# Moving a PSUM copy ahead of a masked score on VectorE, and splitting a wait in front of the products with v

## The chip, the cores and the metric

The kernel runs on one core of a Trainium2 chip. The metric is the device time of one execution in microseconds. Three executions of the kernel before took 3114.57, 3116.45 and 3116.84 us; the median, 3116.45 us, is the time before.

## What is computed

The reference is a chain of four residual blocks on x of 16 sequences x 512 tokens x 256 channels: windowed attention with rotary embedding, an int8 linear layer, a linear attention, and a ternary feed-forward layer with a low-rank term. Only the first block is touched:

```python
q, k, v = split(x @ w_qkv)                    # 16 heads of 64
q, k = l2norm(q) * q_scale, l2norm(k) * k_scale
# windows of 128 queries; each sees the keys of its own, the previous and the next window
q, k = rotary(q * 8), rotary(k)               # rotary(t) = t * cos + rotate_half(t) * sin
sim = where(mask, -max, einsum('bwid,bwjd->bwij', q, k))
out = einsum('bwij,bwjd->bwid', softmax(sim), v) @ w_out
x = layernorm(x + out)
```

## The kernel before

Attention comes first (`run_attention`), sequence by sequence, and takes about 1.93 ms; the other layers follow and share nothing with it in time. The heads are taken in 8 pairs per sequence, 128 pairs in all. A sequence of 512 tokens has four windows (w = 0 to 3) of 128 queries; windows 0 and 3 see 256 keys, windows 1 and 2 see 384. All is fp32.

Every engine runs the same loop, `run_halves`: for each sequence b, each pair p, two halves u = 0 and 1. Half u handles the transposes of the softmax weights of windows w = 2u and w + 1 (global numbers i and i + 1) of its pair, the scores and softmax of the next two windows, and some projections of the pair after the next. Each engine has its own instruction queue, written out by hand: `pe_half`, `act_half`, `dve_half`, `pool_half`. Semaphores tie them together. For one window the work goes like this:

- TensorE computes the scores of both heads h into the PSUM banks SC[w % 2][h] (`pe_scores`, L292).
- VectorE adds the mask, scales, and takes the row extreme (`dve_mask_max`, L518), one instruction per head and a short read of the accumulator. I call it a masked score.
- ScalarE takes the exponential and the row sum (`act_exp`, L420), VectorE the reciprocals of both heads (`dve_reciprocals`, L525), GpSimd multiplies the weights by them (`pool_softmax`, L614).
- TensorE transposes the weights (`pe_transpose_weights`, L309): head 0 into the bank TP, from where ScalarE copies them to pt[0] (`act_evacuate_weights`, L426); head 1 into SC[0][0], or into the bank QK for window 3 of the pairs where `spare` is true (all but p = 0 and 6), from where VectorE copies them to pt[1] (`dve_evacuate_weights`, L530).
- When all four windows of pair n are in pt, TensorE multiplies with v at the head of the next pair's half u = 0 (`pe_values`, L318): 8 products, key block k = 0 to 3 by head, all added up in QK. Key block k needs the weights of windows k - 1 to k + 1 only, but both waits stand ahead of the first product.

Around it, in half u = 0 after the products with v: the next two windows' scores, the transposes of q of the next pair into QK (`pe_q_transpose`, L272; they wait for GpSimd's rotation L598), VectorE's copy of them (`dve_q_evacuate`, L510), the transposes of k into the same bank (`pe_k_transpose`, L279; they wait for that copy), ScalarE's copy of them (L415). VectorE also rotates the projections (`dve_rotate`, L497 and L498, after ScalarE's square L405), sums squares (L503), and, from the second sequence on, takes a maximum for the next layer four times per sequence (`dve_amax`, L548, at the end of halves (p, u) = (2,1), (3,0), (3,1), (4,0)). At (5,1) and (6,1) it takes the low part of the next sequence's x (`dve_x`, L488). `pe_transpose_weights` for head 1 of window w waits until VectorE has read SC[0][0], that is for the masked score (next_i, head 0).

VectorE's order in half u = 1 before the change: rotation (n+2, 1); masked scores (next_i, h 0), (next_i, h 1), (next_i + 1, h 0); copy of window i; masked score (next_i + 1, h 1); reciprocals (next_i); copy of window i + 1; reciprocals (next_i + 1); rotation (n+2, 2).

Of the kernel before, what the change touches and what calls it, by code (L numbers as in the profile page):

```python
# [21 lines left out]
NW = S // WS  # L22
# [15 lines left out]
def semaphores(nc, prefix, *names):  # L38
    return {name: nc.alloc_semaphore(f"{prefix}_{name}") for name in names}

def due(count):
    return not isinstance(count, int) or count > 0
# [4 lines left out]
def halves(t, k):  # L47
    return t[:, 2 * k:2 * k + 2, :].rearrange('p t n -> p (t n)')
# [51 lines left out]
def run_attention(nc, io, mem, psum):  # L100
    SC, TP, PJ, QK = (psum['sc'], psum['tp'], psum['pj'], psum['qk'])

    def spare(i):
        pair, w = divmod(i, NW)
        return w == 3 and pair % PAIRS not in (0, 6)

    def tp_bank(h, i):
        return TP if h == 0 else QK if spare(i) else SC[0][0]
    g = semaphores(nc, 'att', 'x_in', 'x_keep', 'xt_pe', 'xh_act', 'xl_dve', 'pj_pe', 'sq_act', 'rot_dve',
        'rot_pool', 'raw_dve', 'ss_dve', 'rl_act', 'rn_act', 'kn_pool', 'qt_pe', 'qt_dve', 'kt_pe', 'kt_act',  # L110
        'sc_pe', 'sm_dve', 'e_act', 'rc_dve', 'exn_pool', 't_pe', 'pt_act', 'pt_dve', 'pv_pe', 'ot_act', 'op_pe',
        'op_dve', 'y_out', 'w1_act', 'w1_pool', 'scale_in', 'trig_in', 'ident_in', 'wo_in', 'trig_dve', 'zero_pool',
        'mask_pool', 'wh_act', 'wl_pool', 'wl_dve')
# [6 lines left out]
    def span(w):  # L120
        lo, hi = (max(0, w - 1), min(NW - 1, w + 1))
        return lo, hi, (hi - lo + 1) * WS

    def rows(h):
        return slice(h * DH, (h + 1) * DH)

    def pt_keys(h, k):
        lo, hi, width = span(k)
        off = (lo - k + 1) * WS
        return pt[h][:, k, off:off + width]  # L130

    def pt_window(h, w):
        lo, hi, width = span(w)
        first = lo * 3 * WS + (w - lo + 1) * WS
        return pt[h].rearrange('p k n -> p (k n)')[:, first:first + (hi - lo + 1) * 2 * WS].rearrange(
            'p (k n) -> p k n', n=2 * WS)[:, :, 0:WS]

    def blocks(bank, w):
        lo, hi, width = span(w)
        return bank[:, 0:width].rearrange('p (k n) -> p k n', n=WS)  # L140
# [52 lines left out]
    def dve_weights_low(e, k):  # L193
        weights_low(e, k, 1, 'wl_dve')
# [115 lines left out]
        last.then_inc(g['t_pe'], 1)  # L310

    def pe_values(e, n, p):
        e.wait_ge(g['pt_act'], NW * n + NW)
        e.wait_ge(g['pt_dve'], NW * n + NW)
        for k in range(NW):
            lo, hi, width = span(k)
            for h in range(2):
                last = e.matmul(QK[rows(h), lo * WS:(hi + 1) * WS], v[p % 4][:, k, rows(h)], pt_keys(h, k),  # L318
                    start=k == 0, stop=k == NW - 1, skip_group_check=True)
        last.then_inc(g['pv_pe'], 1)  # L320
# [165 lines left out]
    def dve_x(e, seq, k):  # L486
        e.wait_ge(g['xh_act'], 2 * seq + k + 1)
        e.tensor_tensor(token_half(xlo, k), x_bank(seq, k)[:, :].rearrange('p (c n) -> p c n', c=DC),  # L488
            token_half(xhi, k).bitcast(F32), ALU.subtract).then_inc(g['xl_dve'], 1)

    def dve_rotate(e, m, t):
        e.wait_ge(g['sq_act'], TT * m + t + 1)
        if due(TT * m + t - 1):
            e.wait_ge(g['rot_pool'], TT * m + t - 1)
        heads = 'p (k h d) -> p k h d'
        qk = PJ[t % 2][:, 0:2 * PW].rearrange(heads, k=2, h=2)
        e.tensor_tensor(ra[:, t % 2, :].rearrange(heads, k=2, h=2), qk, rotary(t, 0), ALU.mult)  # L497
        last = e.tensor_tensor(rb[:, t % 2, :].rearrange(heads, k=2, h=2), qk, rotary(t, 1), ALU.mult)  # L498
        last.then_inc(g['rot_dve'], 1)

    def dve_norms(e, m):
        e.wait_ge(g['sq_act'], TT * m + TT)
        e.tensor_reduce(ss[:, 0, :], sq[:, :, :].rearrange('p t (h d) -> p (t h) d', d=DH), AX.X,  # L503
            ALU.add).then_inc(g['raw_dve'], 1)
        e.wait_ge(g['raw_dve'], m + 1)
        e.tensor_scalar(ss[:, 1, :], ss[:, 0, :], NORM_FLOOR ** 2, None, ALU.max).then_inc(g['ss_dve'], 1)

    def dve_q_evacuate(e, m, par):
        e.wait_ge(g['qt_pe'], m + 1)
        e.tensor_copy(qT[par][:, :], QK[:, :]).then_inc(g['qt_dve'], 1)  # L510

    def dve_mask_max(e, i, par, w, h):
        lo, hi, width = span(w)
        off = (lo - w + 1) * WS
        e.wait_ge(g['sc_pe'], 2 * i + h + 1)
        if due(2 * i + h - 3):
            e.wait_ge(g['e_act'], 2 * i + h - 3)
        e.tensor_tensor_reduce(out=sm[h][w % 2][:, 0:width], in0=SC[w % 2][h][:, 0:width],  # L518
            in1=mem['mask'][:, off:off + width], scale=rn[:, par,
                4 * w + h:4 * w + h + 1], scalar=3e+38, op0=ALU.add,  # L520
            op1=ALU.min, accum_out=nm[:, w, h:h + 1]).then_inc(g['sm_dve'], 1)

    def dve_reciprocals(e, i, w):
        e.wait_ge(g['e_act'], 2 * i + 2)
        e.reciprocal(rc[:, w, :], rs[:, w, :]).then_inc(g['rc_dve'], 1)  # L525

    def dve_evacuate_weights(e, i, w):
        lo, hi, width = span(w)
        e.wait_ge(g['t_pe'], 2 * i + 2)
        e.tensor_copy(pt_window(1, w), blocks(tp_bank(1, i), w)).then_inc(g['pt_dve'], 1)  # L530

    def dve_residual(e, seq, k):
        e.wait_ge(g['op_pe'], 2 * seq + k + 1)
        if k == 0:
            e.wait_ge(g['x_keep'], 16 * (seq + 1))
            if due(seq):
                e.wait_ge(g['y_out'], 16 * seq)
        e.tensor_tensor(halves(mem['res'], k), QK[:, :], halves(mem['xres'], k), ALU.add).then_inc(g['op_dve'], 1)  # L538

    def dve_stats(e, seq, k):  # L540
        e.wait_ge(g['op_dve'], 2 * seq + k + 1)
        norm.stats(e, seq, mem['res'], (2 * k, 2 * k + 1))

    def dve_amax(e, seq, t):
        if t == 0:
            e.wait_ge(norm.sems['y_act'], seq + 1)
        col = TT * seq + t
        e.tensor_reduce(mem['amax'][:, col:col + 1], mem['res'][:, t, :], AX.X, ALU.max, apply_absolute_value=True)  # L548

    def dve_half(e, at):  # L550
        n, p, u, i, w = (at.pair, at.p, at.u, at.window, at.w)
        ahead, next_i, next_w, par = (at.has_next(), at.next_window, at.next_w, at.next_par)
        out = at.at(0, 1) and not at.first
        if u == 0 and at.has_pair(1):
            dve_rotate(e, n + 1, 3)
            dve_norms(e, n + 1)
        if u == 1 and at.has_pair(2):
            dve_rotate(e, n + 2, 1)
        if not at.first:
            if at.at(1, 0):  # L560
                dve_stats(e, at.b - 1, 1)
        if ahead:
            dve_mask_max(e, next_i, par, next_w, 0)
            dve_mask_max(e, next_i, par, next_w, 1)
        if not at.last:
            if at.at(5, 1):
                dve_x(e, at.b + 1, 0)
            if at.at(6, 1):
                dve_x(e, at.b + 1, 1)
        if u == 0 and at.has_pair(1):  # L570
            dve_q_evacuate(e, n + 1, (p + 1) % 2)
        if ahead:
            dve_mask_max(e, next_i + 1, par, next_w + 1, 0)
        if out:
            dve_residual(e, at.b - 1, 0)
        dve_evacuate_weights(e, i, w)
        if ahead:
            dve_mask_max(e, next_i + 1, par, next_w + 1, 1)
            dve_reciprocals(e, next_i, next_w)
        if out:  # L580
            dve_stats(e, at.b - 1, 0)
            dve_residual(e, at.b - 1, 1)
        dve_evacuate_weights(e, i + 1, w + 1)
        if ahead:
            dve_reciprocals(e, next_i + 1, next_w + 1)
        if at.has_pair(2):
            dve_rotate(e, n + 2, w)
        if at.first and (at.at(0, 1) or at.at(2, 1)):
            dve_weights_low(e, 3 + p // 2)
        if not at.first:  # L590
            for t, step in enumerate(((2, 1), (3, 0), (3, 1), (4, 0))):
                if at.at(*step):
                    dve_amax(e, at.b - 1, t)
# [1324 lines left out]
```

## Time and profile before

| | us |
|---|---|
| median of three executions | 3116.45 |
| the profiled execution | 3117.74 |
| its span | 3115.9 |
| TensorE busy | 2972.7 (95%) |
| VectorE busy | 2360.4 (76%) |
| ScalarE busy | 2164.3 (69%) |
| GpSimd busy | 1658.1 (53%) |
| mean granted TensorE clock | 0.988 of full speed |

The span is one profiled execution from its first instruction to its last; the 1.8 us between it and the execution's own time lie around it. An engine's row in the timeline gives the start, the duration, the line, what is written and read, how many instructions are merged, and in brackets the idle time before it with what ended it. PE is TensorE, PEld its weight loads, DVE VectorE, ACT ScalarE, POOL GpSimd. Successive instructions of one engine overlap a little in the records: on VectorE the next begins some 0.08 us before the end of the one ahead of it.

### The profile page before, as it was taken

Reading aid. Unit: us, or ns where it says so; the run is one execution under the profiler, and the core shown is the slowest. Engines: PE = TensorE matmul, PEld = TensorE weight load, DVE = VectorE, ACT = ScalarE, POOL = GpSimd, SP = SyncE. Lnnn points to the kernel's source line nnn. Section 1 sums busy time; section 2 is a strip of 40 time slices with the busy share of each in tenths; the row PEclk is TensorE's granted clock in tenths of the full one; section 3 lists DMA queues with packets and bytes.
Section 4 is the critical chain, followed back from the end, with each engine's and each line's share of the span. In section 5 each row is a group of like instructions: output and inputs, shape, how many; then the busy total and the mean of one; then the engine's idle time right before and its main releaser. Section 6 shows DMA issues by size and latency. Waiting matters only on the chain. (4 is left out here: it accounts for less than half of the span.)

```text
span 3115.9 us, 56168 instructions
## 1 busy us (share of the span) xinstructions
PE 2972.7 (95%) x18095; PEld 2381.2 (76%) x18095; DVE 2360.4 (76%) x6841; ACT 2164.3 (69%) x5670; POOL 1658.1 (53%) x2226
## 2 busy tenths in 40 slices
PE   7999999999999999999999997699999999999996
PEld 6777777777777777777777775478888888888885
DVE  6877877877877877877877875787777777777775
ACT  5666766766766766765766764477888888888884
POOL 5655655655655654654655654334555555555555
PEclk9999999999999999999999999799999999999998
DMA  2000000000000000000000001200000000000000
GB/s 83 8 15 21 8 15 21 8 15 15 15 15 15 15 15 15 15 15 15 15 15 15 8 21 36 74 14 8 14 15 14 15 21 21 14 15 15 8 15 21
DMA packets 51202, 57.23 MB, mean 18 GB/s; under 512 B 3008, under 2 KB 48592, under 8 KB 50912
## 3 DMA queue, kind: packets, MB, share of 16 engines
q1 hardware_dynamic: 47904, 50.67, 5.0%
q10 hardware_dynamic: 3008, 2.98, 0.3%
q8 instruction: 148, 2.42, 0.3%
q14 instruction: 142, 1.16, 0.1%
HBM read 36.86 MB, written 16.78 MB: 17 GB/s over the span
## 5 line engine op out<-in xcount | busy, mean ns | idle before, releaser
L614 POOL TENSOR_SCALAR a_ex<-a_ex,a_rc 128x384 f32<-128x384 f32 (+1 forms) x1024 | 531.4, 532 | 713.8 <-DVE a_rc L525 713.7
L420 ACT ACTIVATE a_ex<-a_sm,a_nm 128x384 f32<-128x384 f32 (+1 forms) x1024 | 572.2, 560 | 67.3 <-DVE a_nm L518 55.1
L518 DVE CUSTOM_DVE_ANT_0 a_sm<-sc,a_mask,a_rn 128x384 f32<-128x384 f32 (+1 forms) x1024 | 530.4, 544 | 9.3 <-PE sc L292 9.3
L426 ACT ACTIVATE a_pt<-tp 128x256 f32<-128x256 f32 (+1 forms) x512 | 220.0, 430 | 306.4 <-PE tp L309 306.2
L261 PE MATMUL pj<-a_whi,a_xhi 128*128 128x384 f32 x1024 | 391.6, 382 | 7.2 <-DVE a_wlo L187 4.2
L1681 POOL TENSOR_TENSOR b_alo<-b_ring,b_ahi 128x512 fp32r<-128x512 f32 x128 | 169.4, 1323 | 412.0 <-DVE b_ring L1510 373.4
L598 POOL TENSOR_TENSOR a_qr<-a_ra,a_rb 128x256 f32<-128x256 f32 x512 | 369.3, 735 | 12.2 <-DVE a_rb L498 9.0
L261 PE MATMUL pj<-a_whi,a_xlo 128*128 128x384 f32 x1024 | 348.0, 340 | 0.0
L261 PE MATMUL pj<-a_wlo,a_xhi 128*128 128x384 f32 x1024 | 347.2, 339 | 0.0
L292 PE MATMUL sc<-a_kT,a_qT 64*128 64x384 f32 (+1 forms) x2048 | 345.2, 455 | 1.4 <-DVE a_pt L530 0.7
L318 PE MATMUL qk<-a_pt,a_v 128*64 128x384 f32 (+1 forms) x2048 | 303.9, 437 | 26.1 <-DVE a_pt L530 23.9
L318 PEld LDWEIGHTS qk<-a_pt,a_v 128*64 128x64 f32 x2048 | 158.4, 136 | 153.3 <-issue 60.4
L530 DVE COPY a_pt<-sc 128x384 f32<-128x384 f32 (+1 forms) x416 | 210.1, 505 | 85.3 <-PE sc L309 84.7
L292 PEld LDWEIGHTS sc<-a_kT,a_qT 64*128 64x128 f32 x2048 | 176.2, 186 | 122.0 <-issue 80.8
L497 DVE TENSOR_TENSOR a_ra<-pj,a_rot 128x256 f32<-128x256 f32 x512 | 214.6, 419 | 40.5 <-ACT a_sq L405 39.3
L309 PE MATMUL tp<-s_ident,a_ex 128*128 128x128 f32 x1280 | 229.4, 277 | 7.3 <-ACT a_pt L426 6.7
L329 PE MATMUL qk<-a_wo,a_ot 128*128 128x256 f32 x1024 | 228.0, 381 | 1.5 <-DVE a_res L538 0.8
L329 PEld LDWEIGHTS qk<-a_wo,a_ot 128*128 128x128 f32 x1024 | 192.0, 190 | 35.3 <-issue 8.2
L498 DVE TENSOR_TENSOR a_rb<-pj,a_rot 128x256 f32<-128x256 f32 x512 | 212.2, 414 | 0.0
L1477 DVE SCALAR_TENSOR_TENSOR b_ring<-k,b_one_bk,b_ring 128x512 f32<-128x512 f32 x128 | 95.9, 750 | 153.1 <-ACT b_ring L1341 149.9
L261 PEld LDWEIGHTS pj<-a_whi,a_xhi 128*128 128x128 f32 x1024 | 195.3, 191 | 9.7 <-issue 4.7
L606 POOL TENSOR_TENSOR a_qr<-a_qr,a_rn 128x512 f32<-128x512 f32 x128 | 134.5, 1051 | 120.3 <-ACT a_rn L411 120.1
(233 smaller groups left out, 8046.3 us busy)
## 6 DMA issues: line engine op xcount, KB each, us to landing
a_xres<-x SPq DMA_DIRECT2D x16, 512.0 KB, 3.9
y<-a_res SPq DMA_DIRECT2D x16, 512.0 KB, 2.9
b_y<-y SPq DMA_DIRECT2D x16, 512.0 KB, 3.8
a_xin<-x SPq DMA_DIRECT2D x15, 512.0 KB, 4.0
out<-b_y SPq DMA_DIRECT2D x15, 512.0 KB, 2.9
a_xin<-wqkv SPq DMA_DIRECT2D x8, 256.0 KB, 2.8
a_stage<-wqkv SPq DMA_DIRECT2D x3, 384.0 KB, 10.0
a_ot<-wqkv ACTq DMA_DIRECT2D x3, 384.0 KB, 12.5
```

What stands on the lines that cost most here:

```text
L261: last = e.matmul(PJ[t % 2][:, 0:3 * PW], a[:, c, t * P:(t + 1) * P], w[:, c, p * 3 * PW:(p + 1) * 3 * PW], start=c == 0 and k == 0, stop= ...
L292: e.matmul(SC[j][h][:, 0:width], qT[par][rows(h), (w + j) * WS:(w + j + 1) * WS], kT[par][rows(h), lo * WS:(hi + 1) * WS], start=True, sto ...
L309: last = e.transpose(tp_bank(h, i)[:, k * P:(k + 1) * P], ex[h][w][:, k * P:(k + 1) * P], ident[:, :])
L318: last = e.matmul(QK[rows(h), lo * WS:(hi + 1) * WS], v[p % 4][:, k, rows(h)], pt_keys(h, k), start=k == 0, stop=k == NW - 1, skip_group_c ...
L329: last = e.matmul(QK[:, t * DIM:(t + 1) * DIM], ot[:, c, (2 * k + t) * P:(2 * k + t + 1) * P], wo[:, c, :], start=c == 0, stop=c == HC - 1)
L420: e.activation(ex[h][w][:, 0:width], sm[h][w % 2][:, 0:width], ACT.Exp, bias=nm[:, w, h:h + 1], scale=-1.0, accum_out=rs[:, w, h:h + 1]).t ...
L426: e.activation(pt_window(0, w), blocks(TP, w), ACT.Copy).then_inc(g['pt_act'], 1)
L497: e.tensor_tensor(ra[:, t % 2, :].rearrange(heads, k=2, h=2), qk, rotary(t, 0), ALU.mult)
L498: last = e.tensor_tensor(rb[:, t % 2, :].rearrange(heads, k=2, h=2), qk, rotary(t, 1), ALU.mult)
L518: e.tensor_tensor_reduce(out=sm[h][w % 2][:, 0:width], in0=SC[w % 2][h][:, 0:width], in1=mem['mask'][:, off:off + width], scale=rn[:, par, ...
L598: e.tensor_tensor(qr[par][:, t, :].rearrange(half, h=4, s=2), ra[:, t % 2, :].rearrange(half, h=4, s=2), rb[:, t % 2, :].rearrange(half, h ...
L614: e.tensor_scalar(row, row, 0.0, rc[:, w, h:h + 1], ALU.add, ALU.mult).then_inc(g['exn_pool'], 1)
```

## The change

Two edits in `run_attention`. In half u = 1 of the pairs with a spare bank (p = 1 to 5 and 7), VectorE copies window i + 1 right after window i, and the last masked score and both reciprocals follow. In `pe_values`, key blocks 0 and 1 wait for the copies they need, and key blocks 2 and 3 for the last window; where the transposed weights sit in QK, VectorE's copy is still awaited in full ahead of block 0, since the products write that bank.

```diff
     def pe_values(e, n, p):
-        e.wait_ge(g['pt_act'], NW * n + NW)
-        e.wait_ge(g['pt_dve'], NW * n + NW)
         for k in range(NW):
             lo, hi, width = span(k)
+            if k in (0, 2):
+                e.wait_ge(g['pt_act'], NW * n + NW - 1 + k // 2)
+                e.wait_ge(g['pt_dve'], NW * n + (NW if k or spare(NW * n + NW - 1) else NW - 1))
             for h in range(2):
...
         dve_evacuate_weights(e, i, w)
-        if ahead:
+        if ahead and u == 1 and spare(i + 1):
+            dve_evacuate_weights(e, i + 1, w + 1)
             dve_mask_max(e, next_i + 1, par, next_w + 1, 1)
             dve_reciprocals(e, next_i, next_w)
-        if out:
-            dve_stats(e, at.b - 1, 0)
-            dve_residual(e, at.b - 1, 1)
-        dve_evacuate_weights(e, i + 1, w + 1)
-        if ahead:
             dve_reciprocals(e, next_i + 1, next_w + 1)
+        else:
+            if ahead:
+                dve_mask_max(e, next_i + 1, par, next_w + 1, 1)
+                dve_reciprocals(e, next_i, next_w)
+            if out:
+                dve_stats(e, at.b - 1, 0)
+                dve_residual(e, at.b - 1, 1)
+            dve_evacuate_weights(e, i + 1, w + 1)
+            if ahead:
+                dve_reciprocals(e, next_i + 1, next_w + 1)
```

## Rows read from the trace of the kernel before

**Rows 1.** Busy time by stretch: range, length, engines' us (x instructions), clock, DMA share, GB/s.

```profile
400.00:800.00 400.00, 391.30 (x2513) 301.90 (x2512) 310.42 (x1006) 263.78 (x883) 220.45 (x359) 1.00 0.05 16
```

**Rows 2.** TensorE's waits in the first 1900 us: total us, times, longest.

```profile
PE qk L318 <- DVE a_pt L530: 23.2, 95, 0.4
PE qk L279 <- DVE a_qT L510: 9.2, 15, 0.6
```

**Rows 3.** Timeline of TensorE's matmuls where a pair ends and the products with v begin.

```profile
801.64 0.62 PE L318 MATMUL qk<-a_pt,a_v 128*64 128x256 f32 x3 [0.34 <-DVE a_pt L530]
...
812.89 0.38 PE L309 MATMUL qk<-s_ident,a_ex 128*128 128x128 f32 x2
...
813.82 0.34 PE L261 MATMUL pj<-a_wlo,a_xhi 128*128 128x384 f32 x1
814.00 0.34 PE L261 MATMUL pj<-a_whi,a_xlo 128*128 128x384 f32 x1
814.66 0.65 PE L318 MATMUL qk<-a_pt,a_v 128*64 128x256 f32 x4 [0.33 <-DVE a_pt L530]
...
841.32 0.33 PE L261 MATMUL pj<-a_whi,a_xlo 128*128 128x384 f32 x1
841.58 0.65 PE L318 MATMUL qk<-a_pt,a_v 128*64 128x256 f32 x4
```

**Rows 4.** Timeline of VectorE from one such end to the next.

```profile
800.48 0.61 DVE L518 CUSTOM_DVE_ANT_0 a_sm<-sc,a_mask,a_rn 128x384 f32<-128x384 f32 x1
...
802.31 0.42 DVE L497 TENSOR_TENSOR a_ra<-pj,a_rot 128x256 f32<-128x256 f32 x1 [0.27 <-ACT a_sq L405]
...
802.98 0.41 DVE L548 TENSOR_REDUCE s_amax<-a_res 128x1 f32<-128x256 f32 x1
...
806.41 0.68 DVE L510 COPY a_qT<-qk 128x512 f32<-128x512 f32 x1
...
809.95 0.17 DVE L525 RECIPROCAL a_rc<-a_rs 128x2 f32<-128x2 f32 x1 [0.85 <-ACT a_ex L420]
...
813.03 0.55 DVE L530 COPY a_pt<-sc 128x384 f32<-128x384 f32 x1
813.50 0.61 DVE L518 CUSTOM_DVE_ANT_0 a_sm<-sc,a_mask,a_rn 128x384 f32<-128x384 f32 x1
...
814.04 0.16 DVE L525 RECIPROCAL a_rc<-a_rs 128x2 f32<-128x2 f32 x1
814.11 0.40 DVE L530 COPY a_pt<-qk 128x256 f32<-128x256 f32 x1
```

**Rows 5.** Timeline of ScalarE in the same stretch.

```profile
801.13 0.61 ACT L420 ACTIVATE a_ex<-a_sm,a_nm 128x384 f32<-128x384 f32 x1
...
809.30 0.53 ACT L420 ACTIVATE a_ex<-a_sm,a_nm 128x256 f32<-128x256 f32 x1
...
813.81 0.36 ACT L426 ACTIVATE a_pt<-tp 128x256 f32<-128x256 f32 x1
```

**Rows 6.** TensorE's transposes of k, after pairs 3 and 7.

```profile
807.20 0.61 PE L279 MATMUL qk<-s_ident,a_qr 128*128 128x128 f32 x4
...
859.87 0.38 PE L279 MATMUL qk<-s_ident,a_qr 128*128 128x128 f32 x2
```

**Rows 7.** VectorE's copy of q's transposes after pair 7.

```profile
858.74 0.69 DVE L510 COPY a_qT<-qk 128x512 f32<-128x512 f32 x1
```

**Rows 8.** VectorE ahead of a pair's copies in halves with no maximum (L548) near.

```profile
786.98 0.56 DVE L530 COPY a_pt<-sc 128x384 f32<-128x384 f32 x1 [0.29 <-PE sc L309]
...
838.32 0.69 DVE L488 TENSOR_TENSOR a_xlo<-qk,a_xhi 128x512 fp32r<-128x512 f32 x1 [0.16 <-ACT a_xhi L399]
...
852.66 0.56 DVE L530 COPY a_pt<-sc 128x384 f32<-128x384 f32 x1 [0.36 <-PE sc L309]
```

**Rows 9.** GpSimd after pair 3, and TensorE's transposes of q in the last sequence.

```profile
801.28 2.07 POOL L614 TENSOR_SCALAR a_ex<-a_ex,a_rc 128x256 f32<-128x256 f32 x4 [1.71 <-DVE a_rc L525]
...
1885.68 0.55 PE L272 MATMUL qk<-s_ident,a_qr 128*128 128x128 f32 x3 [0.72 <-POOL a_qr L598]
```

## The prediction

> **What bounds the kernel now.** I read the busy time by stretch first: in 400 us of attention TensorE is busy 391 [rows 1], so a removed stall of TensorE looks like time. Then its waits: the longest in total is the one the change aims at, the products with v for VectorE's copy of transposed weights, 23.2 us in 95 waits [rows 2], one for each pair with a spare bank (6 of 8, 96 pairs). Then the timeline of TensorE at a pair's end: from the last projection matmul to the first product it is 814.66 - 814.00 = 0.66 us, against 841.58 - 841.32 = 0.26 after pair 6, where nothing is waited for [rows 3]. So up to 0.40 us is lost at such an end.
>
> Busy shares do not say what sets the period of a pair, so I went through VectorE's and ScalarE's timelines from one pair's end to the next, looking for idle time that TensorE ends. Pairs 3 and 4 are 13.02 us apart (801.64 to 814.66 [rows 3]), and so are two last masked scores (800.48 to 813.50 [rows 4]). Between these two there is a closed chain with next to no slack: masked score at 800.48, its exponential on ScalarE at 801.13 [rows 5], squares behind it, the rotation that waited 0.27 for them (802.31), then VectorE without a pause through the maximum at 802.98 and the copy of q at 806.41 [rows 4], the masked scores around it, ScalarE's exponentials and copies without a pause to 809.30 [rows 5], the reciprocal that waited 0.85 for it at 809.95, and VectorE again without a pause to 813.50 [rows 4]. In this stretch (each sequence but the first has two such periods, ending at pairs 3 and 4) VectorE and ScalarE together set the pace, and TensorE's stall is where it spends what it has to spare. Where no maximum is near, VectorE does wait for TensorE, 0.29 and 0.36 us ahead of the copy [rows 8].
>
> **The change part by part.**
>
> *The copy moves ahead: the gain.* It could begin at 813.50 in place of 814.11, the transposes being done at 812.89 + 0.38 = 813.27 [rows 3, 4]. It then ends 0.61 us earlier and the stall goes whole: 0.40 us here, 0.24 on average over the 95. ScalarE's copy (813.81 + 0.36 = 814.17 [rows 5]) is done in time too, for a product due at 814.26. If nothing else moved, this would be 23.2 us by the waits.
>
> *The masked score moves behind it: the cost.* It starts later by the copy's share of the queue, 0.40 less the overlap of 0.08: **0.32 us** (813.82 for 813.50). Queued behind it are both reciprocals, the rotations, the sum of squares, the next masked scores and the copy of q. The exponential (801.13 there) followed the masked score's end directly, so it is late by 0.32 as well; so are the squares, and the rotation that waits for them. GpSimd, which stood idle 1.71 us for the reciprocal [rows 9], starts 0.32 late and runs on through its rotations.
>
> *What is late next.* The transposes of k wait for VectorE's copy of q. After pair 3 the copy ends at 806.41 + 0.68 = 807.09 and they start at 807.20 [rows 4, 6], 0.11 later; where TensorE really waits for it, 0.06 lies between, so the slack is 0.05 (pair 2 repeats this row). After pair 7 it is 859.87 - 859.43 = 0.44 [rows 6, 7], slack 0.38; pairs 1, 4 and 5 repeat it to 0.03. Hence TensorE may come 0.26 to 0.40 early to the products, but two microseconds on it stands for VectorE.
>
> *The sum over a sequence*, as the shift of TensorE at the transposes of k against now. After pair 1: VectorE +0.32, slack 0.38, so -0.06. Towards pair 2 VectorE's idle time (0.29 and the overlap, 0.37 [rows 8]) takes its shift back to -0.05; the moved copy adds 0.32: +0.27, less slack 0.05: +0.22. Pair 3: nothing in the chain gives way, so +0.27 + 0.32 = +0.59 on VectorE, +0.54 on TensorE. Pair 4: +0.91, less 0.38: +0.53. Pair 5: ahead of the low part of x VectorE has 0.16 + 0.08 idle [rows 8], leaving +0.67; add 0.32, less 0.38: +0.61. Pair 6 has no spare bank and keeps the order: +0.61. Pair 7: VectorE waits for TensorE again (0.36 [rows 8]), +0.61 + 0.32 - 0.38 = +0.55. In pair 0 TensorE's output projection leads everybody, and the count starts anew. That is +0.55 us for each of the 14 middle sequences, 7.7 us. In the last one the transposes of q wait for GpSimd 0.72 us [rows 9] after pair 4, with no slack for the +0.91: 0.9 us. The first has no maxima: six times about -0.02, -0.1. **Sum: +8.5 us**; with rounding of the steps (0.02 each) 8 to 9.5.
>
> *The split wait.* In the pairs with a spare bank block 0 still waits for VectorE's copy in full, and ScalarE's is there in time, so it gives nothing. After pair 0 it could free up to 0.15 us, but there TensorE waits for the copy of q anyway (these are the 15 waits of 0.6 us [rows 2]). After pair 6 nothing waits. Two more waits ahead of block 2 are not in this trace. Below: nothing, as TensorE then stands at the transposes of k. Above: the step of 0.26 into the products, two waits included, is 0.08 over the 0.18 of one projection matmul to the next (813.82, 814.00 [rows 3]); without cover only after pair 6, 16 x 0.08 = 1.3 us. I take 0, the lower end, as TensorE's queue is filled well ahead there.
>
> The profiled execution took 3117.74 us (span 3115.9 and 1.8 around it); the median of the runs is 1.3 below, and I put the sum on the median: 3116.45 + 8.7 = 3125.2 us.
>
> *A rule that speaks for the change.* TensorE's idle gaps lie at these copies [rows 2, 3]. The Trainium skill, Trace Analysis, section Optimization Strategies, says that when the matmul engine is idle waiting for others, the engines that block it are to be optimised. By that rule the wait's 23.2 us would come back and the time would be 3093; it is the first rival below.
>
> **The rivals.**
>
> 1. *Faster: the stall goes and nothing takes its place.* It decides if the copy of q has slack of 0.3 us or more at every pair's end, or if the late exponential is taken in by ScalarE's idle time. For it: TensorE is 98% busy, and after four of six pairs the slack is 0.38. Against: 0.05 after pairs 2 and 3, and the closed chain. Price: -23 us, 3093. Chance 0.08.
> 2. *No change: the chain is looser than I read*, say half of the 0.32 is lost where a wait I took as tight has some room, or the recorded overlap grows. Then pairs 2 to 4 add 0.16 less and the sequence ends near +0.1 or below: -1 to +5 us, 3115 to 3121. For it: the steps are read to 0.01 to 0.03 and there are 20 of them. Chance 0.25.
> 3. *Worse: nothing gives way anywhere*, and each of six moved copies per sequence costs its whole 0.32, as when the delayed GpSimd or the ScalarE queue hits a wait that shows no time now: 6 x 0.32 x 15 = 29 us less what the slack absorbs once, up to 3140. Against: VectorE's idle time of 0.36 by TensorE's doing [rows 8]. Chance 0.10.
> 4. *The split does nothing at all*: holds within each of the cases, as above, and gives no time of its own.
>
> **How the numbers follow.** The forecast has 0.57. A measurement of this kernel can tell about 0.2% from no change, 6.2 us. Slower: the forecast but for its lowest tenth, and case 3, and a little of 2: 0.66. Faster: case 1 and a little of 2: 0.10. Same: 0.24. The range leaves out case 1 and the top of case 3: from case 2's better half, 3113, to 3133. The likeliest case alone: 3122 to 3128.
>
> **What the profile after should show.** VectorE: two copies (L530) in a row at these pairs' ends, the masked score 0.32 us later against the pair's end before. TensorE: the wait of L318 for L530 down from 23 us to under 3, and a wait of L279 for the copy of q up from 9.2 us to some 35 to 50 in about 90 waits. Pairs 2 to 3 and 3 to 4 at 13.34 us apart on VectorE in place of 13.02, pairs 7 and 1 nearly as before. The stage after attention unchanged. I am wrong if L279 waits no longer than now, or if the 13.02 us shrinks: then the chain was not closed.

## The result: 0.68% slower

The changed kernel takes 3136.3 us (median of 6, 3134.0 to 3139.1), the kernel before 3115.9 on the same chips (median of 6): 1.0068 times as long, 95% interval 1.0055 to 1.0081, or 20.4 us. The direction was forecast, but the size was not: 8.7 us were forecast, and 3136.3 lies outside the range of 3113 to 3133. The profiled execution after has a span of 3135.6 us, 19.7 above that of before.

TensorE's waits in the whole of attention (the first 1945 us), after, with the columns of [rows 2]:

```profile
PE qk L272 <- POOL a_qr L605: 24.5, 64, 2.7
PE qk L279 <- DVE a_qT L511: 10.3, 16, 0.7
PE qk L272 <- ACT a_ot L433: 8.8, 15, 0.6
PE sc L309 <- DVE a_nm L519: 5.0, 16, 0.8
...
PE pj L261 <- DVE a_xlo L489: 0.2, 1, 0.2
```

and, for the first of these, the same view of the kernel before:

```profile
PE qk L272 <- POOL a_qr L598: 7.5, 5, 2.3
```

The products with v in the changed kernel; behind the second bar stands the idle time ahead of them:

```profile
L319 PE MATMUL qk<-a_pt,a_v 128*64 128x384 f32 (+1 forms) x2048 | 305.5, 441 | 0.6 <-DVE a_pt L531 0.6
```

The wait that the change aims at is gone: 0.6 us are left in the whole of attention, where it was 23.9 (23.2 of them in the first 1900 us [rows 2]). Waits at the transposes of q (L272) have come up in its place: for GpSimd's rotation, from 7.5 us in 5 waits to 24.5 in 64, and for ScalarE's copy of the products' output, from none to 8.8 us in 15 waits, one in each sequence but the first.

VectorE from the end of pair 3 to that of pair 4, as [rows 4]:

```profile
806.35 0.55 DVE L531 COPY a_pt<-sc 128x384 f32<-128x384 f32 x1
806.82 0.41 DVE L531 COPY a_pt<-qk 128x256 f32<-128x256 f32 x1
807.15 0.61 DVE L519 CUSTOM_DVE_ANT_0 a_sm<-sc,a_mask,a_rn 128x384 f32<-128x384 f32 x1
...
808.55 0.17 DVE L526 RECIPROCAL a_rc<-a_rs 128x2 f32<-128x2 f32 x1 [0.70 <-ACT a_ex L421]
...
813.08 0.68 DVE L511 COPY a_qT<-qk 128x512 f32<-128x512 f32 x1
...
819.71 0.55 DVE L531 COPY a_pt<-sc 128x384 f32<-128x384 f32 x1
820.18 0.41 DVE L531 COPY a_pt<-qk 128x256 f32<-128x256 f32 x1
820.51 0.60 DVE L519 CUSTOM_DVE_ANT_0 a_sm<-sc,a_mask,a_rn 128x384 f32<-128x384 f32 x1
```

and TensorE in it:

```profile
807.33 0.34 PE L261 MATMUL pj<-a_whi,a_xlo 128*128 128x384 f32 x1
807.60 0.65 PE L319 MATMUL qk<-a_pt,a_v 128*64 128x256 f32 x4
...
811.59 0.66 PE L272 MATMUL qk<-s_ident,a_qr 128*128 128x128 f32 x4 [0.34 <-POOL a_qr L605]
...
813.83 0.43 PE L279 MATMUL qk<-s_ident,a_qr 128*128 128x128 f32 x2
...
820.94 0.65 PE L319 MATMUL qk<-a_pt,a_v 128*64 128x256 f32 x4
```

The two copies stand in a row. The first product starts 0.27 us after the last projection matmul (807.60 - 807.33), where it took 0.66 [rows 3]. Both sets of transposes now wait, and k's start 0.07 behind the copy of q (813.83 against 813.08 + 0.68). Two last masked scores are 820.51 - 807.15 = 13.36 us apart, against 13.02 [rows 4]. The period grew by 0.34, as it must where each instruction of the loop waits for the one ahead of it and none has time to spare: the chain was closed.

The shift of TensorE is how much later one of its instructions starts than in the kernel before. I take it from the starts in the two traces at the transposes of k after each pair, with that after pair 0 as zero, in a sequence in the middle:

| after pair | forecast | measured |
|---|---|---|
| 1 | -0.06 | +0.33 |
| 2 | +0.22 | +0.60 |
| 3 | +0.54 | +0.95 |
| 4 | +0.53 | +0.95 |
| 5 | +0.61 | +1.04 |
| 6 | +0.61 | +1.19 |
| 7 | +0.55 | +1.13 |

Between the first products with v and those of the last pair, the 14 middle sequences lose 17.1 us (1.22 each), the last one 3.6, and the first gains 0.7. The rest of the 19.7 us lies outside: 0.3 us lost before the first products, 1.6 lost behind the first products of the last pair, where TensorE's clock fell (last section), and 2.1 gained in the stages after attention. Nothing was changed in those stages; in the profiled executions of the other kernels below they are up to 2.8 us shorter or 2.7 longer than in the one before, so no cause is read from the 2.1.

### The profile page after: what moved, and what is told of

Same layout as the page of the kernel before. It is cut to its first block and busy times, and to the rows that moved or that the text cites. A ratio compares the mean times of both kernels' runs of the same rounds, so it can differ in the third digit from the quotient of the medians.

```text
span 3135.6 us, 56296 instructions
## 1 busy us (share of the span) xinstructions
PE 2986.0 (95%) x18095; PEld 2355.9 (75%) x18095; DVE 2353.8 (75%) x6841; ACT 2164.5 (69%) x5670; POOL 1661.4 (53%) x2226
## 5 line engine op out<-in xcount | busy, mean ns | idle before, releaser
L319 PEld LDWEIGHTS qk<-a_pt,a_v 128*64 128x64 f32 x2048 | 136.8, 137 | 143.3 <-issue 111.8
L526 DVE RECIPROCAL a_rc<-a_rs 128x2 f32<-128x2 f32 x512 | 82.7, 162 | 166.9 <-ACT a_ex L421 166.8
```

## The experiments

Times are compared as ratios to the kernel before, run on the same chip beside them. Its medians there were 3116.05 us (reorder_only, split_only, o_before_apply, not_pair1), 3116.12 (only_pair7, only_pairs23, amax_moved, amax_moved_reorder) and 3117.48 (apply_parted, not_pair5, best).

**The two edits apart: reorder_only and split_only.**

```diff
     def pe_values(e, n, p):
+        e.wait_ge(g['pt_act'], NW * n + NW)
+        e.wait_ge(g['pt_dve'], NW * n + NW)
         for k in range(NW):
-            if k in (0, 2):
...
```

> VectorE's new order alone; both waits stand ahead of the first product with v as before. Theory: the split of the waits gives and costs nothing, the order costs all: 3136 us, within 1.5 of the changed kernel. Rival (the two added waits ahead of key block 2 hold TensorE up): well below the changed kernel, towards 3116 if they are all of it.

Measured: 3140.0 us, 1.0074 (1.0061 to 1.0086). That is 3.7 us above the changed kernel where 1.5 were allowed for, but the two intervals overlap.

The other keeps `dve_half` as it was and has the new `pe_values`.

> The split wait alone, VectorE's order as before. Theory: nothing, 3116 us within 1.5; after pair 0 the products with v start up to 0.15 us early and the transposes of k give it back. Rival (the added waits cost): 3120 or more. Rival (the split gains): the 0.15 us after pairs 0, 3113 or less.

Measured: 3117.2 us, 1.0001 (0.9993 to 1.0010). Its waits in attention:

```profile
PE qk L319 <- DVE a_pt L531: 23.8, 96, 0.6
PE qk L279 <- DVE a_qT L511: 10.3, 16, 0.7
```

All 96 waits stand as before. Within what the times can tell, the order costs all and the split nothing, and the rivals fall. The trace of split_only differs in two places. The products after pair 0 start 0.15 us early and the transposes of k give it back, as expected. And in the last sequence the products after pair 6 waited 0.9 us for ScalarE's copy; the split takes this wait away, and the last pair starts 1.0 us earlier.

**Which pairs cost: only_pair7, only_pairs23, not_pair1, not_pair5.** Each adds a condition to the changed kernel:

```diff
-        if ahead and u == 1 and spare(i + 1):
+        if ahead and u == 1 and spare(i + 1) and p == 7:
```

and `p in (2, 3)`, `p != 1`, `p != 5` for the others.

> The new order after pair 7 only (16 of 96), with the split. Theory: VectorE's and ScalarE's chain has 0.37 us to give there, so the 0.32 is taken in: -0.06 to +0.05 us each, 3116 within 1.5. Rival (each moved copy costs its 0.32 us): 3121.

Measured: 3115.2 us, 0.9997 (0.9988 to 1.0006). VectorE at the end of pair 7:

```profile
850.94 0.56 DVE L531 COPY a_pt<-sc 128x384 f32<-128x384 f32 x1 [0.36 <-PE sc L309]
851.41 0.41 DVE L531 COPY a_pt<-qk 128x256 f32<-128x256 f32 x1
851.74 0.61 DVE L519 CUSTOM_DVE_ANT_0 a_sm<-sc,a_mask,a_rn 128x384 f32<-128x384 f32 x1
```

VectorE has been waiting for TensorE (0.36), as in the kernel before, so here no closed chain runs through VectorE. The delayed masked score is taken in by the slack behind it: the transposes of k after pair 7 come 0.07 early, and a middle sequence takes 0.02 less than before.

> The new order after pairs 2 and 3 only (32 of 96), with the split. Theory: the chain is closed there, both cost in full but for 0.05: the shift is +0.27 after pair 2, +0.59 after pair 3 and stays at 0.59 to the sequence's end, 15 x 0.59 = 9, 3125 us. Rival (cost in proportion, 2 of 6): 3122.5. Rival (TensorE sets the pace there): 3115 or less.

Measured: 3125.3 us, 1.0035 (1.0022 to 1.0047), 0.65 us for each middle sequence. A third of the moved copies makes 9 us and over half of the 1.22 that a sequence loses with all six, so cost goes by place, not by number. After pair 4, which has the old order here, the wait for the copy is back:

```profile
805.35 0.44 PE L319 MATMUL qk<-a_pt,a_v 128*64 128x256 f32 x2
...
819.10 0.44 PE L319 MATMUL qk<-a_pt,a_v 128*64 128x256 f32 x2 [0.33 <-DVE a_pt L531]
```

> The changed kernel with the old order after pair 1 only, the new one after pairs 2, 3, 4, 5 and 7. Theory: pair 1's shift at the transposes of k goes from +0.33 to 0 and the sequence sums to +0.27 (pair 2), +0.59 (3), +0.58 (4), +0.66 (5), +0.80 (6), +0.74 (7): 14 x 0.74 + 3 in the last = 13, 3129 us. Rival (each moved copy costs the same): 5 of 6, 3116 + 17 = 3133.

Measured: 3128.1 us, 1.0043 (1.0029 to 1.0056), the shift 0.00 after pair 1 and 0.26, 0.61, 0.62, 0.71, 0.87, 0.81 after pairs 2 to 7. The rival's 3133 lies just inside the interval, which ends at 3133.5, so the time alone does not exclude it. The trace does: without pair 1's copy a middle sequence loses 0.89 in place of 1.22, so this copy costs 0.33 of it, and not the sixth that the rival gives it.

> The changed kernel with the old order after pair 5 only. Theory: what is late in pair 6's second half is VectorE's low part of the next sequence's x, for which TensorE's projections wait; the shift there falls from VectorE's 1.17 to TensorE's own 0.93, and the sequence ends at 0.9 in place of 1.19: 15 x 0.28 = 4, 3132 us. Rival (pair 5's copy costs what the transposes of k show, 0.1): 3134.5 or more.

Measured: 3133.0 us, 1.0055 (1.0041 to 1.0069), which holds both theory and rival. The shifts decide: a middle sequence loses 1.13 against 1.22 in the changed kernel, not the 0.9 of the theory. After pair 5, with the old order there, TensorE waits for the copy again, by as much as elsewhere:

```profile
836.09 0.44 PE L319 MATMUL qk<-a_pt,a_v 128*64 128x256 f32 x2 [0.34 <-DVE a_pt L531]
```

VectorE was 1.11 us late at that end, and TensorE took the 1.11 from the copy in place of the low part of x. The theory had left this wait out: in a late chain the old order costs as well.

**Why pair 1: o_before_apply and apply_parted.** In the kernel before, ScalarE's layer norm (L92, four instructions) stands ahead of its copy of the products' output at pair 2's start, and the transposes of q write the bank that the copy reads. TensorE and ScalarE there:

```profile
775.86 0.65 PE L318 MATMUL qk<-a_pt,a_v 128*64 128x256 f32 x4 [0.19 <-DVE a_pt L530]
...
779.51 0.63 PE L272 MATMUL qk<-s_ident,a_qr 128*128 128x128 f32 x4
```

```profile
776.80 2.08 ACT L92 ACTIVATE a_res<-a_res,a_ln_shift,a_ln_rs 128x256 f32<-128x256 f32 x4
778.77 0.60 ACT L432 ACTIVATE a_ot<-qk 128x512 f32<-128x512 f32 x1
```

The transposes of q start 0.14 us after that copy's end (779.51 against 779.37) and 3.65 after the first product; at the other pairs it is 3.58. In the changed kernel they start 0.15 after the copy's end, and the wait shows. ScalarE and TensorE:

```profile
782.82 2.08 ACT L92 ACTIVATE a_res<-a_res,a_ln_shift,a_ln_rs 128x256 f32<-128x256 f32 x4
784.79 0.59 ACT L433 ACTIVATE a_ot<-qk 128x512 f32<-128x512 f32 x1
```

```profile
785.53 0.63 PE L272 MATMUL qk<-s_ident,a_qr 128*128 128x128 f32 x4 [0.59 <-ACT a_ot L433]
```

```diff
             if at.at(2, 0) and not at.first:
-                norm.apply(e, at.b - 1, mem['res'])
             if at.has_pair(-1):
                 act_o_evacuate(e, n - 1, (p - 1) % PAIRS)
+            if at.at(2, 0) and not at.first:
+                norm.apply(e, at.b - 1, mem['res'])
```

> The changed kernel, but at pair 2 ScalarE copies the output of the products with v ahead of the layer norm's four instructions, not behind them. Theory: after pair 1 the transposes of q waited for that copy (4.24 us after the first product, 3.65 before the change), so this takes 0.33 to 0.39 us off each of 15 sequences and the time is 3136 - 6 = 3130 us; the transposes of q start there at 3.73, held by GpSimd. Rival (VectorE's chain alone sets that end as well): no change, 3136.

Measured: 3142.2 us, 1.0086 (1.0072 to 1.0100): slower, against the theory and its rival. ScalarE, GpSimd and TensorE after pair 1:

```profile
786.05 0.60 ACT L433 ACTIVATE a_ot<-qk 128x512 f32<-128x512 f32 x1 [0.76 <-PE qk L319]
786.54 2.07 ACT L92 ACTIVATE a_res<-a_res,a_ln_shift,a_ln_rs 128x256 f32<-128x256 f32 x4
788.51 0.20 ACT L410 ACTIVATE a_rl<-a_ss 128x16 f32<-128x16 f32 x1
```

```profile
789.04 1.05 POOL L613 TENSOR_TENSOR a_qr<-a_qr,a_rn 128x512 f32<-128x512 f32 x1 [1.75 <-ACT a_rn L412]
```

```profile
790.23 0.63 PE L279 MATMUL qk<-s_ident,a_qr 128*128 128x128 f32 x4 [0.73 <-POOL a_qr L613]
```

The layer norm now stands ahead of the key norms (L410), GpSimd's scaling of k waits for these, and the transposes of k for GpSimd: a shift of +0.74 after pair 1. The four instructions take 2 us, ScalarE had 0.76 idle ahead of the copy. So part them:

```diff
             if at.at(2, 0) and not at.first:
-                norm.apply(e, at.b - 1, mem['res'])
+                norm.apply(e, at.b - 1, mem['res'], (0, 1), done=False)
             if at.has_pair(-1):
                 act_o_evacuate(e, n - 1, (p - 1) % PAIRS)
+            if at.at(2, 0) and not at.first:
+                norm.apply(e, at.b - 1, mem['res'], (2, 3))
```

> The changed kernel, with the layer norm's four instructions on ScalarE parted: two ahead of its copy of the output of the products with v, two behind it. The whole four behind it held up the norms of k (transposes of k 0.88 us behind the copy of q in that run); whole ahead they hold up the transposes of q. Theory: parted they hold up neither, pair 1's shift falls from +0.33 to -0.06 at the transposes of k and the sequence from 1.19 to 0.8: 15 x 0.39 = 6, 3130 us. Rival (the shift after pair 1 comes from VectorE's chain): 3136.

Measured: 3130.0 us, 1.0043 (1.0031 to 1.0056), against 1.0068 for the changed kernel. The shifts after pairs 1 to 7 are -0.08, 0.24, 0.60, 0.61, 0.70, 0.85, 0.80. ScalarE and TensorE:

```profile
780.86 1.10 ACT L92 ACTIVATE a_res<-a_res,a_ln_shift,a_ln_rs 128x256 f32<-128x256 f32 x2
781.84 0.61 ACT L433 ACTIVATE a_ot<-qk 128x512 f32<-128x512 f32 x1
782.32 1.10 ACT L92 ACTIVATE a_res<-a_res,a_ln_shift,a_ln_rs 128x256 f32<-128x256 f32 x2
```

```profile
783.06 0.66 PE L272 MATMUL qk<-s_ident,a_qr 128*128 128x128 f32 x4
```

With this one wait out of the way the forecast's table holds to 0.09 as far as pair 5 (-0.06, 0.22, 0.54, 0.53, 0.61). The copy of q tells the same: after pair 1 it ends 0.47 us ahead of the transposes of k in the kernel before and in the changed one alike, so that slack is not used there, and with the layer norm parted it ends 0.06 ahead. This is the largest term that was missing.

**Is the chain what sets the pace: amax_moved, amax_moved_reorder, best.**

```diff
-            for t, step in enumerate(((2, 1), (3, 0), (3, 1), (4, 0))):
+            for t, step in enumerate(((2, 1), (4, 0), (7, 0), (7, 1))):
```

> The kernel before, with the four maxima per sequence at the ends of halves (2,1), (4,0), (7,0) and (7,1) in place of (2,1), (3,0), (3,1), (4,0): nothing on TensorE changes. Theory (VectorE and ScalarE set the two periods of 13.02 us): each goes to the 12.72 of a period without maxima, and the moved ones are taken in where there is room: 15 x 0.6 = 9, 3107 us. Rival (TensorE sets the pace, VectorE is 76% busy): 3116.

Measured: 3106.4 us, 0.9973 (0.9963 to 0.9984). The first products after pairs 2, 3 and 4:

```profile
782.94 0.44 PE L318 MATMUL qk<-a_pt,a_v 128*64 128x256 f32 x2 [0.19 <-DVE a_pt L530]
...
795.65 0.44 PE L318 MATMUL qk<-a_pt,a_v 128*64 128x256 f32 x2 [0.19 <-DVE a_pt L530]
...
808.38 0.44 PE L318 MATMUL qk<-a_pt,a_v 128*64 128x256 f32 x2 [0.19 <-DVE a_pt L530]
```

They are 12.71 and 12.73 us apart, with the same instructions on TensorE and as many on VectorE, in other halves. In these two periods VectorE and ScalarE set the pace, though VectorE is busy 76% of the time.

> The changed kernel with the maxima moved as in the run before. Theory: the order still costs, since without maxima the chain of a period is 12.37 + 0.32 = 12.69 us and with one 13.02, against TensorE's 12.46: slower than the kernel with the maxima moved alone by 12 to 18 us, 3119 to 3125. Rival (the two periods with maxima were all that made the order cost): no slower than that kernel, 3107 or less.

Measured: 3130.2 us, 1.0049 (1.0036 to 1.0063), 24 us above amax_moved. The order costs at least as much here as on the kernel before, and more than the 12 to 18 expected. By the shifts a middle sequence loses 1.5 us against amax_moved. Of these, 0.33 come after pair 1, which the expectation lacked, and 0.28 after pair 7, where the changed kernel loses nothing: two maxima now stand at that pair. That they and the delayed masked score need the same slack is the likely reason, but no run shows it.

> Meant to beat both: VectorE's old order and the old waits, the maxima moved to (2,1), (4,0), (7,0), (7,1), and the layer norm parted on ScalarE. Theory: the 9 to 10 us of the moved maxima, and 15 x 0.07 = 1 us more as the transposes of q after pair 1 start 3.58 after the first product in place of 3.65: 3105 us. Rival (parting disturbs the norms of k): 3107 or more.

Measured: 3109.1 us, 0.9972 (0.9963 to 0.9981). It and amax_moved beat both kernels by 0.3%, and are the same within their intervals: the parting gives nothing measurable by itself. The transposes of q after pair 1 do come 0.07 earlier, those of k do not.

## Why the prediction missed

1. *The gain* (the stall goes whole): right. L318's wait fell from 23.9 us to 0.6. But the time did not fall with it: some 4 us after the first product TensorE now stood for GpSimd, and 2 us after that for VectorE's copy of q. The Trainium skill, Perfetto Trace Analysis, section Optimization Strategies, says to optimise the engines that block the critical path when the matmul engine waits for them. Reordering VectorE's queue did not do that: it took the wait away and the time rose by 20 us. Where VectorE was relieved on the chain (amax_moved), the time fell by 9.7 us as the rule has it, with 19.5 us of the wait still there.
2. *The masked score moves by 0.32 us, and what is queued behind it*: right. Masked scores, exponentials and rotations all show it; the period went from 13.02 to 13.36, where 13.34 was forecast. only_pairs23 (3125.3 against 3125) and only_pair7 (3115.2 against 3116) confirm the places with no room and with room.
3. *After pair 1*: wrong, and the largest error. The step said that pair 1 "repeats" pair 7 to 0.03 in the slack of the transposes of k. So it does, but there the transposes of q start 3.65 us after the first product in place of 3.58, held by ScalarE's copy behind the layer norm. That wait had no room at all, and I had read only the slack at the transposes of k. Measured +0.33, forecast -0.06; apply_parted, where the wait is gone, has -0.08.
4. *Towards pair 2*: wrong as a consequence. VectorE's idle time of 0.37 was to take its shift back; but it ends when TensorE is there, and TensorE was itself late by 0.33. Pairs 2 to 5 carry 0.38 to 0.43 more than forecast, 14 x 0.39 = 5.5 us; apply_parted and not_pair1 take 0.33 a sequence of it out (0.89 in place of 1.22).
5. *Pair 6*: wrong by 0.15. I let VectorE's idle time at the copy (0.02 and the overlap) absorb the rest, but TensorE waits earlier, for the low part of x and for a masked score. In the changed kernel TensorE, then VectorE:

```profile
845.01 0.52 PE L309 MATMUL sc<-s_ident,a_ex 128*128 128x128 f32 x3 [0.26 <-DVE a_nm L519]
845.58 0.41 PE L309 MATMUL tp<-s_ident,a_ex 128*128 128x128 f32 x2
845.92 0.44 PE L261 MATMUL pj<-a_whi,a_xhi 128*128 128x384 f32 x1
```

```profile
845.18 0.69 DVE L489 TENSOR_TENSOR a_xlo<-qk,a_xhi 128x512 fp32r<-128x512 f32 x1
```

   The projection starts 0.05 after the low part's end (845.87). TensorE's weight loads (PEld) show the wait, once in each sequence that has a next one:

```profile
PEld pj L261 <- DVE a_xlo L489: 2.8, 15, 0.4
```

   In the kernel before, and in not_pair5, it is one wait of 0.2 us. So the wait is real, but its price of 0.15 a sequence, 14 x 0.15 = 2.1 us, is the shift's growth in this pair and was not shown by an edit: not_pair5 removed the wait and put the copy's in its place.

6. *The last sequence*: 3.6 us in place of 0.9. The GpSimd wait went from 0.7 to 1.4 us, and 1.2 us were lost by the end of pair 5; the other 2.4 came in the next pair with TensorE's clock (below).
7. *The split* gives nothing: right within the noise. "After pair 6 nothing waits" was wrong for the last sequence, where split_only gained 1.0 us.
8. *The signs to look for*: the wait was to appear at the transposes of k, 35 to 50 us. It appears two microseconds earlier, at those of q, for GpSimd, which the text had named as late and not priced. At k's it is mostly under the pipelined matmuls and not counted as idle: it shows at the weight loads for them, 24.4 us in 48 waits for the copy of q where it was 13.6 in 16.

Together: 17.1 us in the middle sequences against 7.7 forecast is 5.5 (pair 1), 2.1 (pair 6), 0.5 in steps of a few hundredths, and 14 x 0.09 = 1.3 between the table's +1.13 and the 1.22 of a whole sequence, which was not followed up. The forecast's 8.7 us is itself 0.2 above the 8.5 that its terms add up to; no row stands for the 0.2.

Of the rivals, the third (nothing gives way) named the right kind of miss, "a wait that shows no time now", and 3136 lies in its 3140 and below; but only_pair7 shows that its mechanism is not general. The measured case is the forecast's with one more closed wait after pair 1, a smaller loss in pair 6, and a fallen clock in the profiled execution.

## What to carry to other kernels

When an instruction is moved on a queue that is not the busiest, look for the closed chain: follow each instruction back to what released it until the same place comes round one period earlier; if no link has room, a delay of 0.3 us costs 0.3 us per period, whatever the busy shares say. Ends that look alike in one slack can differ in another, so check for each of them every wait between the edit and the next meeting of the engines; here the sign was 0.07 us in the trace before, 3.65 in place of 3.58 from the first product to the transposes of q. The way to the gain was to take work off the chain (the maxima, 0.3%), not to change the order in it.

## What was not expected of the hardware

TensorE's granted clock fell in the last sequence of the changed kernel's profiled execution. Busy time by stretch, the clock third from the end of a row:

```profile
1910.00:1915.00 5.00, 5.00 (x37) 3.48 (x35) 3.83 (x15) 4.44 (x15) 4.27 (x8) 1.00 0.18 52
1915.00:1920.00 5.00, 3.02 (x21) 2.16 (x20) 4.96 (x13) 2.87 (x9) 3.61 (x4) 0.94 0.23 57
1920.00:1925.00 5.00, 4.26 (x18) 2.69 (x17) 2.04 (x10) 2.39 (x7) 3.34 (x5) 0.50 0.00 0
1925.00:1930.00 5.00, 4.67 (x28) 2.71 (x30) 2.33 (x8) 3.56 (x12) 1.89 (x4) 0.88 0.19 52
...
1935.00:1945.00 10.00, 8.37 (x38) 5.54 (x38) 0.98 (x2) 1.71 (x4) 3.04 (x4) 0.83 0.01 2
```

In 1920 to 1925 it was half, the lower of its two levels (1.2 in place of 2.4 GHz), after a stretch in which TensorE was busy 3.02 of 5 us. The eight score matmuls took 2.50 us there and 1.35 at the full clock:

```profile
1922.45 2.50 PE L292 MATMUL sc<-a_kT,a_qT 64*128 64x256 f32 x8 [0.74 <-DVE a_pt L531]
...
1929.78 1.35 PE L292 MATMUL sc<-a_kT,a_qT 64*128 64x384 f32 x8
```

The period from pair 5's end to pair 6's is 2.4 us longer there than before, while in apply_parted, with the same instructions on TensorE and the full clock, it is 0.4 shorter: the fall cost 2.8 us. A second fall, in 1935 to 1945, cost 1.6. Before, TensorE was as idle in the place of the first and the clock stayed:

```profile
1898.00:1903.00 5.00, 2.88 (x24) 2.02 (x21) 4.59 (x14) 3.68 (x12) 3.03 (x5) 1.00 0.17 54
```

The profiled execution of reorder_only has the first fall too (0.66 over 1920 to 1930), but not the second. No other profiled execution has either: the granted clock is 1.00 in that place in all eleven. The last sequences of apply_parted, not_pair1, not_pair5 and o_before_apply lose 0.4 to 1.2 us against 3.6 and 4.0. How busy TensorE is in this place does not tell them apart: in the 6 us from the first product after pair 5, it was busy 4.68 us in the changed kernel and 4.69 in apply_parted. I tried nothing to provoke or prevent the fall, so what decides it stays open, and so does how often it happens in the executions without a profile.
